# A two-layer sandwich kernel on eight cores: the PSUM ring advanced in front of a turn, and a row sum with a weight load moved behind the first Wk2 tile

## The reference

```python
x = x + _layernorm(_L0_attn_ref(_layernorm(x), Wq, Wk, Wv, Wo, norm_w))
x = x + _layernorm(_L0_ffn_ref(_layernorm(x), W_r, W_k, W_v, mu_r, mu_k))
```

## Time and profile before

| | |
|---|---|
| median of 3 runs | 2648.62 us (2647.23 to 2648.83) |
| profiled execution, its own time | 2647.15 us |
| its span on the slowest core (core 4) | 2645.4 us |
| spans of the eight cores | 2637.6 to 2645.4 us |
| mean granted TensorE clock, each core | 0.996 |
| TensorE busy | 2593.5 us, 98% |
| VectorE, ScalarE, GpSimd busy | 48%, 42%, 16% |

### The profile page before, as it was taken

The page is one execution under the profiler, slowest core; times in us unless marked ns, Lnnn a source line. Parts: engine busy times, 40 slices in busy tenths (PEclk is TensorE's granted clock), DMA queues, the critical chain, the costliest instruction groups (busy, mean ns, idle before and its releaser), DMA issues.

```text
span 2645.4 us, 53094 instructions; the slowest of 8 cores (2637.6 to 2645.4 us)
## 1 busy us (share of the span) xinstructions
PE 2593.5 (98%) x19384; PEld 1753.8 (66%) x19528; DVE 1271.7 (48%) x2119; ACT 1114.8 (42%) x1325; POOL 412.6 (16%) x351
## 2 busy tenths in 40 slices
PE   7999999999999999999799999999999999999998
PEld 6678877777778887776465565556655565556654
DVE  5544544444544444434554544445444544445443
ACT  5755656555656566554332222222222222222221
POOL 0412333322222233332000000000000000000000
PEclk9999999999999999999899999999999999999999
DMA  7032223333332222344321100110011100110000
GB/s 235 17 97 81 92 84 106 97 97 97 97 89 79 83 73 70 91 133 142 110 81 49 49 33 25 41 49 33 33 41 41 49 33 25 41 49 36 31 24 25
DMA packets 118224, 181.89 MB, mean 69 GB/s; under 512 B 74960, under 2 KB 75216, under 8 KB 117968
## 3 DMA queue, kind: packets, MB, share of 16 engines
q1 hardware_dynamic: 117968, 178.49, 21.4%
HBM read 98.25 MB, written 65.54 MB: 62 GB/s over the span
## 4 chain that ended last, share of the span: by engine, by line
PE 86%; ACT 4%; DVE 3%; DMA 2%; POOL 2%; issue 2%; SPq 1%; DVEq 0%; ACTq 0%; POOLq 0%
PE ps L272 48%; PE ps L289 31%; PE ps L669 3%; PE ps L609 1%; PE ps L634 1%; DMA ln_scr<-lnp 1%; PE ps L944 1%; PE ps L313 1%; DVE st L324 1%; DMA xt<-xN 1%; SPq L484 1%; POOL ebk L562 1%; DMA wst<-woT 1%; POOL kt_l L570 0%; POOL ebk L573 0%
## 5 line engine op out<-in xcount | busy, mean ns | idle before, releaser
L289 PE MATMUL ps<-xk_h,wk 128*128 128x256 bf16 x2048 | 339.6, 273 | 0.0
L289 PE MATMUL ps<-lnh,wq 128*128 128x256 bf16 x1920 | 319.3, 273 | 1.6 <-ACT kf L492 1.6
L289 PE MATMUL ps<-lnh,wk 128*128 128x256 bf16 x1920 | 316.9, 273 | 0.0
L272 PE MATMUL ps<-wo,o_h 128*128 128x512 bf16 x1038 | 312.5, 381 | 2.0 <-issue 0.4
L272 PE MATMUL ps<-wv,lnh 128*128 128x512 bf16 x1024 | 307.1, 379 | 2.5
L272 PE MATMUL ps<-wv,kc_h 128*128 128x512 bf16 x1007 | 300.9, 379 | 1.8 <-DVE ln2T L936 0.3
L272 PE MATMUL ps<-wr,xr_h 128*128 128x512 bf16 x994 | 298.1, 379 | 1.1 <-DVE x L923 0.2
L289 PE MATMUL ps<-xk_l,wk 128*128 128x256 bf16 x1024 | 280.0, 273 | 0.0
L289 PE MATMUL ps<-lnl,wq 128*128 128x256 bf16 x960 | 261.7, 273 | 0.0
L289 PE MATMUL ps<-lnl,wk 128*128 128x256 bf16 x960 | 261.7, 273 | 0.0
L329 POOL TENSOR_TENSOR aa<-v,mhalf 128x1 f32<-128x1 f32 x98 | 53.7, 548 | 1122.2 <-DVE v L327 1122.2
(11 more groups left out here) (146 smaller groups left out, 4390.5 us busy)
## 6 DMA issues: line engine op xcount, KB each, us to landing
xt<-xN SPq DMA_DIRECT2D x16, 1024.0 KB, 6.5
x<-xN SPq DMA_DIRECT2D x16, 1024.0 KB, 4.8
outN<-x SPq DMA_DIRECT2D x32, 512.0 KB, 2.6
ln_scr<-lnp SPq DMA_DIRECT2D x14, 1024.0 KB, 9.2
oh_scr<-os_h SPq DMA_DIRECT2D x16, 512.0 KB, 5.7
ol_scr<-os_l SPq DMA_DIRECT2D x16, 512.0 KB, 6.3
o_h<-oh_scr SPq DMA_DIRECT2D x14, 512.0 KB, 3.4
o_l<-ol_scr SPq DMA_DIRECT2D x14, 512.0 KB, 4.5
```

The lines of the kernel that those rows point to most:

```text
L272: op("tensor", lambda e, xo=xo, wo=wo, ci=ci, first=first, last=last: e.matmul(bank[:], xo[:, ci, js], wo[:, ci, hs], start=first, stop=last),
L289: last=last: e.matmul(bank[:, os], wo[:, ci, ds], xo[:, ci, ts], start=first, stop=last),
```

## The change

It adds a step of two to the ring in front of `turn_chunk(0)`, and it takes `gla_rms(L, 1)`, the event for `rf` and the fetch of Wv2 out of the hand-written stretch and puts them behind `wk2_tile(1)` in the loop. With that `load_o(3)` comes in front of the fetch. The arithmetic is the same.

```diff
@@ -1088,6 +1088,7 @@
     wo_chunk(1, 1, got)
     gla_scores(L, 1)
     bt["xr_mm"] = bt["kc_mm"] = [ev("T")]
+    ring_n[0] += 2
     turn_chunk(0)
     got = wo_mm(2, 0)
     turn_chunk(1)
@@ -1098,18 +1099,18 @@
     store_o(L)
     ring_n[0] += 3
     last = wo_mm(2, 1)
-    gla_rms(L, 1)
     bt["xr"] = mix(mur, xr_h, xr_l, bt["xr_mm"])
     wo_chunk(2, 0, got)
     wo_chunk(2, 1, last)
-    evg = [ck[L]["rms"], o_ev[L]]
-    bt["rf"] = [[ck[L]["rms"]]] * 2
-    fetch_pair("wv2", *evg)
     load_o(3)
     bld.flush()
     for q in range(1, nt):
         more = q + 1 < nt
         wk2_tile(q)
+        if q == 1:
+            gla_rms(L, 1)
+            bt["rf"] = [[ck[L]["rms"]]] * 2
+            fetch_pair("wv2", ck[L]["rms"], o_ev[L])
         if more and q > 1:
             wo_chunk(q + 1, 0)
             wo_chunk(q + 1, 1)
```

## The result

The changed kernel takes 2655.69 us (median of 15 runs), the kernel before 2649.1 us (15 runs beside them). The ratio is 1.0023, 95% interval 1.0014 to 1.0032: slower, by some 6 us (3.7 to 8.5), close to what a measurement can tell from no change. Some executions of every kernel are longer because cores of a die were granted a lower clock (0.84 to 0.94 in four of the changed kernel's 15 runs, which the ratio leaves out, and mostly 0.97 to 0.985 in the experiments). The profiled execution has a span of 2653.8 us on core 4, against 2645.4 in the earlier trace rows; its busy times are those of before.

The account below looks back on a forecast made before the run. TensorE's own work was taken to set the second half's pace. +6.6 us at the end of `wo_mm(2, 0)`, -0.3 for `rv`, +1.8 of clock, -0.4 for short waits gave +7.7; forecast 2656.0 us, range 2652.5 to 2659.0.

Parts of the forecast that it names:

- The count of banks: Counted from calls of `take`: the turn gets free banks 6, 7; `wo_mm(2, 0)` gets 0, 1, held until `A_l L620`.
- in the second half a microsecond reaches the end whole: Between the halves, each microsecond gained or lost moves the end equally, since only TensorE's work sets the second half's pace.
- The start of the Wo job: `wo_mm(2, 0)` waits 12.4 us for `A_l L620`, replacing a 5.97 us pause, and starts 5.05 us late.
- The clock behind the long pause: In `wo_mm(2, 0)`, low clock after the 12.4 us wait costs 2.4 us; bounds 1.8 and twice 2.4.
- The Wk2 tile: Wk2's first tile, no longer behind the row sum, starts after `rv`, 4.9 us late instead of 6.6.
- The Wr pause: The second Wr job waits for `wo_chunk(2, 1)`'s first bank: a new 3.1 us pause, start 6.3 us late.
- Its clock: Low clock in the Wr jobs behind the new 3.1 us pause costs 1.8 us; lower bound 0.
- No wait for `rv` at the last turn: The last turns' fourth bank, freed by `rv`, is free in time; without the clock's loss, 0.9 us of wait.
- none for Wv2: Wv2's transfers, issued later at 1344.6, land by 1361.7, before first use at 1372: no wait.
- The two short waits: Short waits of 0.27 us at 1364.36 and 0.1 in front of it are covered: -0.4 us in the sum.
- The row sum's own worth: Moving the row sum starts Wk2's tile 1.7 us sooner on TensorE, but the gain is lost in the Wr tile.
- The rule of the Trainium skill: Transposes do not count as busy like matmuls: about 1.1 us less clock loss, sum +6.6 instead of +7.7.

Follow-up runs that it names:

- e1: The kernel before with only the ring step of two added, row sum and Wv2 fetch left in place: 6.4 us slower from first turn to end, ratio 1.0038.
- e11: e6 without the moved row sum and fetch: 0.9 us faster than the kernel before from first turn to end, ratio 1.0039.
- e2: The changed kernel without the ring step, only row sum and fetch moved: 0.9 us slower than before from first turn to end, ratio 0.9998.
- e4: e3 with the moved row sum and fetch added: 2.8 us faster than the kernel before from first turn to end, ratio 0.9894.
- e6: The changed kernel with `gla_scores(L, 1)` put in front of `wo_chunk(1, 1, got)`: 0.7 us faster than the kernel before from first turn to end, ratio 0.9985.
- e9: The kernel before, banks of first turn and Wo job swapped, each later bank named: 0.4 us faster from first turn to end, ratio 1.0025.
- e3: The kernel before with `wo_mm(2, 0)` issued in front of `turn_chunk(0)`, each on its old banks: 3.1 us faster from first turn to end, ratio 0.9893.

## Why the prediction was right

The forecast was 2656.0 us; the median is 2655.69. That these are 0.3 us apart is luck in part. The difference was forecast as 7.7 us and is 6.1 by the ratio (3.7 to 8.5), 7.1 by A. The medians of the runs that the ratio uses are 2654.55 and 2648.92. What holds is the path: a bank that comes back with `A_l`, a pause in the Wr tile behind it, and Wv2 in time. By its steps, in the mean of eight cores where not said otherwise:

- **The count of banks** holds: the wait for `A_l L620` is on every core. So does **"in the second half a microsecond reaches the end whole"**: Wv2 starts 7.14 us later (112.26 behind the first turn, not 105.12), the end comes 7.1 us later.
- **The start of the Wo job** was to be 5.05 us late and is 5.7 (36.1, not 30.4). The row at 1289.54 in the earlier trace rows lacks the record of its first matmul, as the single one there shows, and I read it as the start; cores with both records start it 1.8 us behind the turn's start, which on core 4 is 1289.1. The new row at 1296.46 lacks one in the same way, which makes 12.75 us of a wait that is 12.4 on six other cores.
- **The clock behind the long pause** was to cost 2.4 us. The job took 12.0 us against 10.35 at full clock, 1.7 lost; cores between 1.3 and 2.1. These two misses cancel, which is luck: the end was forecast +6.6 and is +6.4.
- **The Wk2 tile** was to start +4.9 and starts +4.7, behind `rv`, at full clock.
- **The Wr pause** was to be 3.1 us and is 2.6 on all cores; the second Wr job on core 4 is 5.7 us late, not 6.3. This is the term I mis-sized: I took 0.3 us off VectorE's chain for the removed `rv`, and from the first `rv` to the second chunk's `x L923` it is 0.8 us shorter (28.48 us, not 29.25). 0.4 lie between that `rv` and the first `xr_l`, where `rv` was removed. The other 0.4 lie at one place: in front of the second chunk's `bb` (L343) VectorE stands 0.46 us on every core of before, e1 and e11, and 0.11 on every core of the changed kernel, e2, e4 and e6. So it goes with the moved row sum; what VectorE waits for there no view names.
- **Its clock** was to cost 1.8 us: from the second Wr job to the turns 17.22 us on every core, 15.5 at full clock, 1.7 lost. A pause of 2.33 us at full clock, my argument for a lower bound of 0, was a weaker sign than I took it for: on cores 2 and 6 of the same execution the same pause (2.33 and 2.28 us) brought the clock to half. In e1, where there is no such pause, Wr to Wv2 takes 23.0 us as before; in the changed kernel 26.9.
- **No wait for `rv` at the last turn**, and **none for Wv2**: both hold. The load is issued at 1346.0 and 1346.6, and lands in at most 13.9 us, 12 us ahead of its use.
- **The two short waits** in front of Wv2, 0.4 us in the sum, gave 0.2: from the last turns to Wv2 it is 1.8 us, before 2.0. With the terms above the sum as measured is 6.4 - 0.8 + 1.7 - 0.2 = 7.1.
- **The row sum's own worth**: I said that the tile's early start "doesn't last", and e2 and e4 show it: the pause goes 25 us further on and takes 1.7 us of clock with it, +0.9 by A.
- **The rule of the Trainium skill** that I weighed (TensorE: Matmul & The Clock Gate, part 4, PE-mode transpose), that transposes don't count as busy in the way matmuls do, would have had the long pause lose about 1.1 us less than my 2.4, some 1.3. Measured are 1.3 to 2.1, mean 1.7. Two shorter pauses are nearer to a test: the one of 5.97 us, which ended in transposes, lost 1.9 us in the mean of the eight cores of before, and the one of 5.1 us in e9, which ended in the Wo job itself, 2.0. They show no sign of the 1.1 us, but as the pauses differ in length they don't settle the rule.

The view of the landings in the changed kernel's first Wv2 load:

```profile
DMA to landing us min/median/max: 8.8/11.3/13.9
```

## What to carry to other kernels

When a ring of buffers is advanced to spare one step a held buffer, list who gets each buffer behind it: the next taker may have to wait for a release that stands much further back in another engine's queue. Ask which step in the pause is the longest and give that one the free buffers; here the Wo job first was worth 3 us, the turn first lost 7. And a pause moved in front of another release by the same engine is not removed, only made later, and it may then cost clock where it did not stand before.

## What the runs showed of the hardware

- A pause of 12.4 us cost no more clock than one of 5.97 us: 2.1 us on core 4 (0.17 of a window that is 12.4 us long too) against 2.1 for the shorter one on the same core, and 1.7 against 1.9 in the mean of eight, although it is twice as long. The low level held for the first part of the job and then full clock came back, in both.
- Behind a short pause the clock fell or stayed, and its length did not decide which. Every core has a pause of 1.1 to 2.3 us near 66 us. At 2.33 us it left core 4 of before at full clock and brought core 2 of the same execution, and core 4 of the changed kernel, to half. Their windows, in this order:

```profile
68.50:71.00 2.50, 2.50 (x25) 2.28 (x24) 1.56 (x4) 2.10 (x3) 0.00 (x0) 1.00 0.00 0
68.50:71.00 2.50, 2.50 (x14) 1.94 (x13) 1.39 (x3) 2.10 (x3) 0.00 (x0) 0.53 0.34 48
68.50:71.00 2.50, 2.50 (x13) 2.08 (x12) 1.57 (x4) 2.10 (x3) 0.00 (x0) 0.50 0.00 0
```

- In the stretch of the change, 1.78 us in front of the Wk2 tile left the clock at full on all eight cores, and 2.57 us in the Wr tile brought it to half for a while on all eight. But in e6 two of the six cores kept full clock behind a 2.6 us pause there, and in e9 three of six behind the 3.25 us in front of the row sum. In e3 a pause of 2.05 us was followed by the turn's transposes and the row sum at full clock, with three gaps of 0.2 to 0.5 us, and then by a stretch at 0.56. Its windows on core 3:

```profile
1294.10:1295.00 0.90, 0.63 (x4) 0.44 (x5) 0.69 (x1) 0.70 (x2) 0.00 (x0) 1.00 0.00 0
1296.10:1300.00 3.90, 3.90 (x44) 3.90 (x42) 2.00 (x1) 1.33 (x3) 0.00 (x0) 0.56 0.01 4
```

There the matmuls of 128x128 come every 0.107 us, and at full clock every 0.056. For the price of a moved pause this means that 2 to 3 us of idleness can be free on one core and cost 1.7 us on another: one core's row doesn't settle it, and all eight should be read.
